# Cutting the expert stages on TensorE in halves and giving the biases a stage, with every engine's order laid out anew

## What is computed

```python
h = _layernorm(x) * (1 + ca) + sa                      # ca, sa, ga, ... from silu(c) @ wmod
x_dbl = einsum('bld,ed->ble', h, W_x)                  # 64 columns dt, 16 B, 16 C
dt = softplus(einsum('blr,dr->bld', dt_raw, W_dt) + b_dt)
A_bar = exp(dt[..., None] * -exp(A_log)); dB_u = (dt * h)[..., None] * B_sel
h_t = A_bar_t * h_(t-1) + dB_u_t                       # 16 states for each channel
x = x + ga * (einsum('bldn,bln->bld', h_t, C_sel) + h * D_param)
g = _layernorm(x) * (1 + cb) + sb
gates = top2(softmax(g @ Wg)), normalised
x = x + gb * sum_e gate_e * (g @ We[e] + be[e])
```

## Time and profile before

| | us |
|---|---|
| median of 3 runs | 1220.47 |
| the profiled execution | 1216.74 |
| its span | 1214.9 |
| before the first `mul` | 49.4 |
| from the first `mul` to the end of the last scan | 1053.5 |
| after it | 112.0 |

### The profile page before, as it was taken

The page is one execution under the profiler, slowest core; times in us unless marked ns, Lnnn a source line. Parts: engine busy times, 40 slices in busy tenths (PEclk is TensorE's granted clock), DMA queues, the critical chain, the costliest instruction groups (busy, mean ns, idle before and its releaser), DMA issues. The chain is left out here.

```text
span 1214.9 us, 13519 instructions
## 1 busy us (share of the span) xinstructions
PE 932.1 (77%) x4235; PEld 590.9 (49%) x4235; DVE 1023.8 (84%) x826; ACT 715.2 (59%) x1412; POOL 1001.4 (82%) x357
## 2 busy tenths in 40 slices
PE   5335444578878888698877898788968897789998
PEld 4101111245644556455554565355644565456786
DVE  2399999999899989998999989998999989995110
ACT  4864569556874669557865588466955367331200
POOL 1376676689997999799997999799979999797453
PEclk9656766599998998999998999898998999889899
DMA  5607160364427171555346261727144443611132
GB/s 164 155 19 168 40 138 1 89 173 101 125 70 208 46 190 36 135 145 134 92 104 175 65 169 46 171 91 182 52 114 132 113 115 84 166 45 47 57 100 61
DMA packets 90552, 131.21 MB, mean 108 GB/s; under 512 B 13536, under 2 KB 73512, under 8 KB 90480
## 3 DMA queue, kind: packets, MB, share of 16 engines
q1 hardware_dynamic: 90480, 130.34, 41.2%
HBM read 54.50 MB, written 8.65 MB: 52 GB/s over the span
## 5 line engine op out<-in xcount | busy, mean ns | idle before, releaser
L965 POOL TENSOR_TENSOR h<-h,Cr 128x2048 f32<-128x2048 f32 x129 | 582.4, 4517 | 97.0 <-DVE h L835 53.5
L835 DVE TENSOR_TENSOR_SCAN h<-av,ps 128x1024 f32<-128x1024 f32 x256 | 584.7, 2284 | 16.6 <-DVE ps L828 0.9
L588 PE MATMUL ps<-xg,we 128*128 128x256 f32 x2048 | 501.1, 401 | 21.3 <-POOL xg L1002 18.9
L588 PEld LDWEIGHTS ps<-xg,we 128*128 128x128 f32 x2048 | 402.0, 201 | 119.1 <-POOL xg L1002 33.8
L1002 POOL TENSOR_TENSOR xg<-h2T,gbc 128x1024 f32<-128x1024 f32 x128 | 304.3, 2383 | 64.8 <-DMA gbc<-gates 30.7
L828 DVE TENSOR_TENSOR ps<-ps,dd 128x1024 f32<-128x1024 f32 x256 | 315.4, 1232 | 46.7 <-PE ps L473 26.1
L631 ACT ACTIVATE av<-dd,An 128x1024 f32<-128x1024 f32 x256 | 289.5, 1141 | 69.7 <-DVE h L835 50.9
L492 PE MATMUL ps<-h,gam 128*32 128x512 f32 x1024 | 141.2, 674 | 44.1 <-POOL h L965 33.4
L685 ACT ACTIVATE Cr<-ps 128x512 f32<-128x512 f32 x64 | 38.0, 596 | 99.8 <-PE ps L533 79.9
L473 PE MATMUL ps<-S,sel 64*128 64x512 f32 x128 | 51.7, 487 | 48.3 <-DVE ps L828 48.3
L492 PEld LDWEIGHTS ps<-h,gam 128*32 128x32 f32 x1024 | 29.2, 117 | 119.8 <-issue 77.4
(11 more groups left out here) (100 smaller groups left out, 855.9 us busy)
## 6 DMA issues: line engine op xcount, KB each, us to landing
dd<-src SPq DMA_DIRECT2D x512, 128.0 KB, 2.4
gbc<-gates SPq DMA_DIRECT2D x128, 256.0 KB, 3.7
X<-in_x SPq DMA_DIRECT2D x8, 1024.0 KB, 8.2
out<-X SPq DMA_DIRECT2D x32, 256.0 KB, 3.3
XN<-in_x SPq DMA_DIRECT2D x7, 1024.0 KB, 7.9
we<-in_We SPq DMA_DIRECT2D x2, 1024.0 KB, 8.7
XN<-in_x SPq DMA_DIRECT2D x2, 512.0 KB, 5.2
Cr<-in_wmod SPq DMA_DIRECT2D x1, 1024.0 KB, 5.3
```

Source lines behind the costliest of these rows:

```text
L588: e = pe.matmul(bk[:, m * 256:(m + 1) * 256], we[:, hf, 2 * ep + e2, m * P:(m + 1) * P], xg[:, i % XG, e2, hf], start=(ep == e2 == m == hf ...
L835: dve.tensor_tensor_scan(h[:, u % HS], av[:, u % AS], wide(BP), 0.0, ALU.mult, ALU.add).then_inc(s_scan, 1)
L965: pool.tensor_tensor(hu, hu, Cr[:, q:q + 1].to_broadcast([P, n, L]), ALU.mult).then_inc(s_ch, n)
```

## The change

- A pair's stage is cut in two, one for each expert (`e2`). The second half signals `s_f` as before; the wait for `xg` and for the chunk's bank stands in the first half.
- The biases are a stage of their own (`biases`) with a semaphore of its own (`s_fb`), on which `fE` and the DMA `gr` now wait.
- `AT` has new values throughout, and two more (`fh`, `fb`). The due times of the new stages follow from them.

No instruction of work is added or removed. Sorting the due times gives these orders, old against new, around the points that the prediction speaks of (where an engine isn't named it is TensorE):

- `f.3.1.3`, biases, `Bs.40`, `C.5.3.0`, `f.3.2.0`, `C.5.3.1`, `o.3.1`, `y.39` becomes first half of `f.3.1.3`, `Bs.40`, second half, biases, `C.5.2.0`, first half of `f.3.2.0`, `C.5.2.1`, second half, `o.3.1`, `y.39`. `C.5.3.0` and `C.5.3.1` come after `f.3.2.2`. The same holds in each of blocks 1 to 5.
- VectorE: `oX.b.0`, `oX.b.1`, `zs`, the first `zX` and one `corr` of each block stand one `mul` earlier than before. Where before they stood between a `mul` and its scan, they now stand after the scan before it. In block 7 `mul.238` comes after `soft.6` and `top.6`, not ahead of them. Everything else on VectorE stays.
- GpSimd: two swaps in a block (one `xg` with a `dt` step, one `xg` with a `ch`), with nothing waited for in between.
- ScalarE: the copy of the last quarter of `hT` comes after one more `exp` (`exp.179` in block 5).
- SyncE: `gw` and the first `gl` come after the `ddu` that stood behind them (`ddu.15.2` for `gw.6`/`gl.6.0.0`), and `gl.7.2.3` comes ahead of `out.7.1`.
- In the last block `z.7.0` stands between two halves, `lg.7.0` and `lT.7.0` on either side of a half, and `o.7.2` comes after the last biases, not ahead of `f.7.3.3`.

```diff
-AT = dict(exp=0.41, mul=-0.14, scan=0.75, ch=8.26, Bs=0.81, y=7.93, stat0=-4.62, stat0s=0.74, rstd0=1.29,
-          rsb0=0.84, xh0=4.13, xh0s=0.3, xT0=15.39, xT0h=1.43, xTs=2.34, rxT0=0.24, wx=4.22, rwx=1.64, S=0.01,
-          ldx=29.86, gam=19.72, dl0=20.66, dl1=36.03, dls=3.26, rdl=0.66, corr=0.19, dt=7.52, C=25.68, CS=2.8,
-          Cc=0.74, rC=0.39, ddt=37.96, ddts=1.56, ddu=38.08, ddus=2.02, zs=2.87, ldx2=31.09, z=5.08, zX=-0.99,
...
+AT = dict(fh=0.19, fb=0.52, exp=0.38, mul=0.14, scan=0.58, ch=8.08, Bs=0.71, y=8.02, stat0=-2.88, stat0s=0.34,
+          rstd0=1.38, rsb0=0.0, xh0=2.05, xh0s=0.78, xT0=15.25, xT0h=1.11, xTs=3.01, rxT0=0.51, wx=4.5,
+          rwx=1.59, S=-0.32, ldx=33.84, gam=19.37, dl0=20.92, dl1=36.13, dls=3.04, rdl=0.67, corr=0.15,
+          dt=7.74, C=25.66, CS=4.2, Cc=0.41, rC=0.71, ddt=37.96, ddts=1.34, ddu=38.47, ddus=1.26, zs=3.12,
...
-            put(s + times["f"], "f", b, c, ep)
+            put(s + times["f"], "f", b, c, ep, 0)
+            put(s + times["f"] + AT["fh"], "f", b, c, ep, 1)
         s += times["f"]
+        put(s + AT["fh"] + AT["fb"], "f", b, c, E // 2, 0)
...
-                        sp.wait_ge(s_f, 16 * b)
+                        sp.wait_ge(s_fb, 4 * b)
...
-                _, b, c, ep = s
+                _, b, c, ep, e2 = s
                 i = 16 * b + 4 * c + ep
-                pe.wait_ge(s_xg, i + 1)
-                if i == 0:
+                if e2 == 0:
+                    pe.wait_ge(s_xg, i + 1)
+                if i == e2 == 0:
                     left(pe, FB)
                     pe.wait_ge(s_we, 32)
                 bk = ps[:, expert_bank(b, c)]
-                if ep == 0 and b == LAST and c in (1, 2):
+                if ep == e2 == 0 and b == LAST and c in (1, 2):
                     pe.wait_ge(s_zr, 2 * b + 2)
-                elif ep == 0 and 4 * b + c:
+                elif ep == e2 == 0 and 4 * b + c:
                     pe.wait_ge(s_fe, 4 * b + (1 if b == LAST and c == 3 else c))
-                for e2 in range(2):
-                    for m in range(2):
-                        for hf in range(2):
-                            e = pe.matmul(bk[:, m * 256:(m + 1) * 256], we[:, hf, 2 * ep + e2, m * P:(m + 1) * P],
-                                          xg[:, i % XG, e2, hf], start=(ep == e2 == m == hf == 0), stop=False)
-                if ep == E // 2 - 1:
-                    if b == LAST and c >= 2:
-                        pe.wait_ge(s_grB, 16)
-                    else:
-                        pe.wait_ge(s_gr, 16 * (b + 1))
-                    for m in range(2):
-                        e = pe.matmul(bk[:, m * 256:(m + 1) * 256], beb[:, m * P:(m + 1) * P],
-                                      gT[:, 256 * c:256 * c + 256], start=False, stop=(m == 1))
-                e.then_inc(s_f, 1)
+                for m in range(2):
+                    for hf in range(2):
+                        e = pe.matmul(bk[:, m * 256:(m + 1) * 256], we[:, hf, 2 * ep + e2, m * P:(m + 1) * P],
+                                      xg[:, i % XG, e2, hf], start=(ep == e2 == m == hf == 0), stop=False)
+                if e2:
+                    e.then_inc(s_f, 1)
+
+            def biases(b, c):
+
+                if b == LAST and c >= 2:
+                    pe.wait_ge(s_grB, 16)
+                else:
+                    pe.wait_ge(s_gr, 16 * (b + 1))
+                bk = ps[:, expert_bank(b, c)]
+                for m in range(2):
+                    e = pe.matmul(bk[:, m * 256:(m + 1) * 256], beb[:, m * P:(m + 1) * P], gT[:, 256 * c:256 * c + 256],
+                                  start=False, stop=(m == 1))
+                e.then_inc(s_fb, 1)
...
-                    expert(s)
+                    expert(s) if s[3] < E // 2 else biases(s[1], s[2])
...
-                    act.wait_ge(s_f, 4 * (i + 1))
+                    act.wait_ge(s_fb, i + 1)
```

More of the change, by code:

```diff
@@ new lines @@
+AT = dict(fh=0.19, fb=0.52, exp=0.38, mul=0.14, scan=0.58, ch=8.08, Bs=0.71, y=8.02, stat0=-2.88, stat0s=0.34,
+          rstd0=1.38, rsb0=0.0, xh0=2.05, xh0s=0.78, xT0=15.25, xT0h=1.11, xTs=3.01, rxT0=0.51, wx=4.5,
+          rwx=1.59, S=-0.32, ldx=33.84, gam=19.37, dl0=20.92, dl1=36.13, dls=3.04, rdl=0.67, corr=0.15,
+          dt=7.74, C=25.66, CS=4.2, Cc=0.41, rC=0.71, ddt=37.96, ddts=1.34, ddu=38.47, ddus=1.26, zs=3.12,
+          ldx2=36.35, z=4.84, zX=-1.23, zd=2.87, stat1=6.49, stat1s=0.38, rstd1=9.41, rsb1=1.03, xh1=11.08,
+          xh1s=0.0, xh1g=2.33, xT1=11.82, xT1h=0.31, xT1s=1.48, rxT1=0.38, lg=13.63, rlg=1.15, lT=0.91,
+          soft=0.54, softe=1.41, top=0.63, gT=2.12, rgT=0.31, gw=11.92, gr=34.65, xg=23.29, xgs=1.78,
+          gl=-2.82, f=-3.11, fE=0.98, o=2.13, oX=1.45, out=15.41, md1=-55.67, gates=-54.23, ga=-19.89,
+          bn0=-119.77, bn0s=24.67, stat1A=4.67, stat1B=12.15, stat1sA=6.44, stat1sB=4.34, rstd1A=3.23,
+          rstd1B=9.54, rsb1A=4.03, rsb1B=0.2, xh1A=7.75, xh1B=25.71, xh1sA=0.0, xh1sB=11.71, xh1gA=21.4,
+          xh1gB=5.82, xT1A=9.47, xT1B=55.12, xT1hA=0.0, xT1hB=14.92, xT1sA=5.91, xT1sB=23.25, rxT1A=-0.98,
+          rxT1B=16.11, lgA=10.26, lgB=95.62, rlgA=-0.56, rlgB=-3.23, lTA=0.59, lTB=5.54, softA=3.32,
+          softB=-2.86, softeA=-2.65, softeB=4.97, topA=4.25, topB=13.47, gTA=3.12, gTB=20.82, rgTA=-1.86,
+          rgTB=9.14, gwA=29.25, gwB=32.11, grA=68.42, grB=130.47, xgA=47.64, xgB=167.51, xgsA=10.58,
+          xgsB=8.35, glA=2.59, glB=15.41, fA=26.64, fB=-6.18, fEA=73.01, fEB=38.22, oA=23.31, oB=80.07,
+          oXA=13.37, oXB=73.95, outA=46.61, outB=74.52, stat1P=6.43, stat1sP=0.42, rstd1P=9.38, rsb1P=0.0,
+          xh1P=10.02, xh1sP=0.0, xh1gP=2.43, xT1P=11.96, xT1hP=0.01, xT1sP=1.76, rxT1P=-0.29, lgP=14.18,
+          rlgP=-0.43, lTP=0.14, softP=-0.51, softeP=0.27, topP=-0.16, gTP=1.39, rgTP=-1.04, gwP=10.7,
+          grP=38.07, xgP=21.33, xgsP=1.82, glP=-4.41, fP=-2.77, fEP=0.53, oP=4.34, oXP=9.43, outP=68.77)
@@ L303, in adaln_block @@
         s_zt, s_zr = sem("s_zt"), sem("s_zr")
-        s_xg, s_f, s_fe = sem("s_xg"), sem("s_f"), sem("s_fe")
+        s_xg, s_f, s_fb, s_fe = sem("s_xg"), sem("s_f"), sem("s_fb"), sem("s_fe")
         s_am, s_v = sem("s_am"), sem("s_v")
```

## The result

The kernel after takes 1224.93 us (median of 6 runs, 1223.10 to 1226.19), the kernel before in the same measurement 1217.43 (1215.72 to 1220.68). The ratio is 1.0057, with a 95% interval from 1.0040 to 1.0074: about 7 us slower. The forecast was 1216.7, faster. The time lies at the upper end of the range, where rival 1 had put it (1224.6), but that is partly luck: the forecast started from 1220.47, 3.0 above the later median, and rival 1's +4.1 on 1217.43 would be 1221.5. The profiled execution's span is 1222.5 us, 7.6 more than before's.

A forecast was written before the change was run, and what follows sets the result against it. Before the tail, GpSimd's packed loop through `soft` was taken as bounding, nearly equal to VectorE's; TensorE bounds the tail. Terms -2.8 - 1.5 + 1.5 + 0 - 1.0 = -3.8 us gave 1216.7, range 1209 to 1225.

The forecast's parts named there:

- rival 1: Clock stays low in `f.x.2.0`, VectorE reaches `soft` 0.6 late in six blocks: +4.1 us, 1224.6; chance 0.24.
- The boundary wait: VectorE's wait for `Bs` at the starts of blocks 2 to 7 is removed: 2.34 here, 16.0 over six by itself.
- The gain at `soft`: VectorE comes 1.1 early, but only the slack at six `soft`, 3.4 less 0.1 per signal, is won: -2.8 us.
- GpSimd's 0.29: GpSimd's wait at 724.10 for the end of `f.3.2.1` goes, 0.3 in each of five blocks: -1.5 us.
- What is given back behind `soft`: After `soft` VectorE is the bound; the sums end later and `zs` waits 0.3 in five blocks: +1.5 us.
- The first block: Head of the kernel: SyncE's order of the first transfers, for which the first `mul` wait, is unchanged: 0.
- Block 6 to the last scan: First `gl` and `xg` of block 6 come 1.3 later, the third pair's 1.23 of waiting goes: sum 0.
- The tail: After the last scan, waits of 0.62 and 0.70 go and 0.3 is lost around the last pair: -1.0 us.
- Rival 2: VectorE alone is the bound, so the six boundary waits go in full: -16.0 - 1.0, 1203.5; chance 0.08.

The follow-up runs named there:

- gl_early: Kernel after with one SyncE step undone, the first pair's gates copy of block 6 ahead of the `ddu` group again: ratio 1.0064 to before.
- boundary: Kernel after with all old orders, except `Bs` of the first pair in blocks 1 to 6 between halves of the preceding expert stage: ratio 0.9992 to before.

## Why the prediction was wrong, point by point

- **The boundary wait**: right, in place and size. `oX.3.1` waits 0.95, forecast 1.0; four of the six blocks have 0.95 to 0.97 and two, where the clock was low, 2.21 and 2.56, for which I had 2.7. That half a stage in this stretch speaks for the higher clock held in four of six blocks, in before it was high in two.
- **The gain at `soft`**, -2.8: this is the step that failed, together with the next. VectorE is early there, but not by the 1.1 us that I had: in block 5 it waits 0.38 and 0.61 at two `Bs` on the way, and then 0.26 for `lT` (0.26 to 0.44 in four blocks). `soft` starts 0.04 behind the end of `lT` (0.33 before), so the slack was used. But `lT` itself came 89.49 us after GpSimd's wait for the scan, not 89.24 as in the earlier trace rows, because GpSimd's stretch to the end of its last `xg` is 84.95 us long, not 84.70. Of 0.47 a block 0.04 was left in block 5. (The six slacks listed are those of blocks 1 to 6; the first `soft` had none, it waited 0.32.)
- **GpSimd's 0.29**, -1.5: wrong. The wait for the expert stage went from there, and one of 0.67 for the gates' copy came at 719.60. In SyncE's order a `ddt` group now stands ahead of the copy `gl.3.2.1`, and the write `out.3.0` closer ahead of it; that this makes the copy late is read off the order, no run tests it. I had followed SyncE's queue only in block 6 and behind it. With the two blocks of low clock, these two terms of together -4.3 came out at +1.0.
- **What is given back behind `soft`**, +1.5: right in kind, too small, +3.4. The stretch takes 43.8 to 44.2 instead of 43.36 in five blocks: 0.4 to 0.9 a block, not 0.3. I had priced ScalarE's swap ahead of the sums and taken TensorE's order behind `soft` as unchanged.
- **The first block**: missed, +2.6 at the first `soft`. I had costed a swap on ScalarE at nothing because in the middle blocks GpSimd's last `xg` hides it. In block 0 there is none, and the swap costs 1.05; the other 1.5 I cannot name.
- **Block 6 to the last scan**, 0: measured +2.1. Both terms came as forecast (the copy 1.4 later, forecast 1.3; the third pair's wait gone), but the first `xg` came 2.1 later behind `soft`, and gl_early shows that the copies behind it form one queue.
- **The tail**, -1.0: right within what can be told, -1.5 in this profile and about -1 over all.
- **Rival 2** (the six waits go in full, -16) is refuted by `boundary`. By the rule that I had drawn from the Trainium skill, "Perfetto Trace Analysis" (section "Optimization Strategy"), these 16 us would have been won. The trace does not bear that out: VectorE's gaps went from `Bs` (16.0 to 0.7) to `oX` (13.0), and the gain was at most 3.2.
- **Rival 1** gave the right time largely by luck. Its low clock came in two of six blocks, which hold +2.7 us ahead of `soft`; in `boundary` it came in four, and in three of these the stretch to `soft` is within 0.02 of before's. Most of the rest, behind the `soft` and ahead of the first one, it did not have.

The forecast's mistake as a whole is the sum over places looked at. Where several loops are of nearly one length, a place that gets shorter gains little and a place that gets longer costs, so that the small terms left out tend to one sign. That is my reading; no run here tests it.

## What to carry to other kernels

Before removing a wait, measure the same stretch to the next meeting of the engines and ask whether anything else ends there; here one experiment with six moved steps would have told that the wait only moves. Price each swap in the block where nothing hides it, most often the first and the last. A step that is taken earlier is free only as long as its input has slack at the lowest clock that its producer runs at.

## What the runs showed of the hardware

The granted clock differs from run to run of one kernel, and the time goes with it. In 28 runs of before on one chip the mean clock was from 0.857 to 0.887 and the time from 1224.7 to 1213.2 us, about 3.5 us less for each 0.01 (correlation -0.94). Which is the cause these runs do not tell. Inside one execution of before, blocks 2 and 5 have the same orders and the same work but took 134.5 and 132.9 us. The lines are the two blocks, and then the same 12 us of each, 40 us after its start:

```profile
309.80:444.30 134.50, 113.06 (x528) 72.07 (x529) 126.08 (x95) 90.71 (x185) 125.59 (x42) 0.92 0.46 120
710.20:843.10 132.90, 111.20 (x524) 71.51 (x524) 126.07 (x95) 90.57 (x185) 124.32 (x42) 0.94 0.46 120
349.80:361.80 12.00, 9.04 (x43) 5.14 (x44) 11.52 (x8) 6.38 (x10) 12.00 (x5) 0.86 0.30 67
750.20:762.20 12.00, 7.44 (x44) 4.67 (x44) 11.52 (x8) 6.37 (x9) 12.00 (x5) 1.00 0.35 80
```

The clock falls to the lower of its levels at another place of the block (0.86 against 1.00 in the last two lines), and the block has another length. The six runs of after lie at 0.864 to 0.869, so part of its 7 us may be that its order brings the low clock to places where it hurts. An estimate from a straight line through the 28 runs: they would be at 1220.9 for a clock of 0.867, and the six runs of after lie 2.2 to 4.9 above the line. By it some 3 us go with the clock and some 4 do not, so the clock alone (rival C of the single steps) is not the whole difference. No run here held the clock and changed the order, and the split stays open.
